# A block table inside the expert loop: gathers and stores by token, queries from SBUF to SBUF, and filler matmuls

## The reference

```python
x = x + gelu(layernorm(x) @ ctx.T) @ ctx                     # 1: context as weights
# 2: eight experts, every token goes to one of them
probs = softmax(xt @ Wg)                                     # xt = layernorm(x), 2048 tokens
top_idx = top_k(probs.T, cap=256)                            # each expert picks 256 tokens
tok2exp = best of the experts that picked the token, or the best of all
out = sum_e where(tok2exp == e, weight, 0) * (gelu(xt @ W1[e]) @ W2[e])
x = x + out
# 3: attention of ctx (keys, values) and layernorm(x) (queries), 16 heads of 16, masked, relative bias
x = x + attention(q = layernorm(x) @ Wq, k = ctx @ Wk, v = ctx @ Wv) @ Wo
# 4: per batch one of eight experts is chosen from the last token, then
x = x' + 0.3 * (expert(x') @ Wo + bo)                        # x' = layernorm(x)
```

## Time and profile before

| | |
|---|---|
| median of 3 runs | 817.16 us (813.94 to 817.80) |
| profiled execution, its own time | 816.39 us |
| its span in the trace | 814.6 us |
| PE busy | 682.0 us, 84% |
| DVE, ACT, POOL busy | 352.0, 271.2, 34.9 us |
| mean granted TensorE clock | 0.904 of full |
| HBM read, written | 50.12 MB, 20.79 MB |

### The profile page before, as it was taken

How to read it: one execution, slowest core, us unless ns; L and a number is a source line. 1 busy time by engine, 2 the same in 40 slices (tenths; PEclk the granted TensorE clock), 3 DMA queues, 4 the chain that set the end, 5 groups by cost and what they waited for, 6 DMA issues and landing times.

```text
span 814.6 us, 8616 instructions
## 1 busy us (share of the span) xinstructions
PE 682.0 (84%) x2992; PEld 370.3 (45%) x2993; DVE 352.0 (43%) x965; ACT 271.2 (33%) x371; POOL 34.9 (4%) x40
## 2 busy tenths in 40 slices
PE   4999999999777226999727888999999998978997
PEld 2666666666554114666512332333333345444455
DVE  4414320030356201222255666777777844525134
ACT  1111111111132101334215313665666654752410
POOL 0000000000100430000070000000000000000000
PEclk9999999999989757999957765999999989989999
DMA  9974019120011153211136931035035100022102
GB/s 312 363 245 169 0 56 375 61 84 0 1 48 48 55 170 99 64 52 60 57 100 119 160 65 41 1 74 105 17 65 114 28 2 1 1 73 83 52 27 77
DMA packets 53547, 71.76 MB, mean 88 GB/s; under 512 B 8498, under 2 KB 46290, under 8 KB 52322
## 3 DMA queue, kind: packets, MB, share of 16 engines
q1 hardware_dynamic: 51970, 67.04, 29.4%
q0 software_dynamic: 1536, 4.20, 1.6%
HBM read 50.12 MB, written 20.79 MB: 87 GB/s over the span
## 4 chain that ended last, share of the span: by engine, by line
PE 66%; DVE 15%; issue 6%; DMA 5%; ACT 4%; SPq 3%; POOL 0%; DVEq 0%; ACTq 0%
PE ps L753 12%; PE ps L764 11%; PE ps L1190 7%; PE ps L1104 6%; DVE arena L1811 6%; PE ps L1171 5%; PE ps L913 4%; DMA arena<-xs_sorted 4%; PE ps L1239 3%; PE ps L1228 3%; PE ps L931 3%; PE ps L726 3%; PE ps L962 2%; PE ps L1251 2%; DVE arena L1592 1%
## 5 line engine op out<-in xcount | busy, mean ns | idle before, releaser
L1811 DVE TENSOR_REDUCE arena<-ps 128x1 f32<-128x416 f32 x256 | 140.7, 587 | 57.3 <-PE ps L1104 54.8
L1407 ACT ACTIVATE arena<-ps 104x1024 f32<-104x1024 f32 x128 | 124.4, 1020 | 81.1 <-PE ps L1171 81.0
L753 PE MATMUL ps<-xnT,arena 128*128 128x512 f32 x208 | 102.4, 618 | 0.9 <-DVE xnT L1477 0.9
L764 PE MATMUL ps<-arena 128*128 128x256 f32 x416 | 98.9, 382 | 0.0
L1104 PE MATMUL ps<-arena 97*128 97x416 bf16 x256 | 88.4, 378 | 11.8 <-DVE arena L1811 5.6
L764 PEld LDWEIGHTS ps<-arena 128*128 128x128 f32 x416 | 80.0, 192 | 33.4 <-issue 25.0
L1278 ACT ACTIVATE arena<-ps 128x512 f32<-128x512 f32 x52 | 31.0, 597 | 175.3 <-PE ps L753 175.3
L1171 PE MATMUL ps<-arena 100*104 100x512 bf16 x256 | 80.8, 405 | 2.3 <-ACT arena L1407 2.2
L1190 PE MATMUL ps<-arena 104*32 104x512 f32 x512 | 71.2, 629 | 0.2 <-ACT arena L1407 0.2
L1104 PEld LDWEIGHTS ps<-arena 97*128 97x128 bf16 x256 | 23.4, 101 | 105.5 <-DVE arena L1811 93.1
L1477 DVE COPY xnT<-ps 128x512 f32<-128x512 f32 x32 | 21.0, 687 | 111.6 <-PE ps L726 111.6
(11 more groups left out here) (186 smaller groups left out, 659.8 us busy)
## 6 DMA issues: line engine op xcount, KB each, us to landing
arena<-in_W SPq DMA_DIRECT2D x16, 512.0 KB, 9.4
arena<-in_ctxT SPq DMA_DIRECT2D x4, 1664.0 KB, 8.1
arena<-in_ctxN SPq DMA_DIRECT2D x4, 1664.0 KB, 13.3
arena<-q_parts SPq DMA_DIRECT2D x48, 128.0 KB
arena<-in_pW SPq DMA_DIRECT2D x8, 512.0 KB, 4.5
xs_sorted<-zero_tile_s SPq DMA_DIRECT2D x1, 3328.0 KB, 20.1
ys_sorted<-zero_tile_s SPq DMA_DIRECT2D x1, 3072.0 KB, 24.5
q_parts<-arena SPq DMA_DIRECT2D x24, 128.0 KB, 1.8
```

What stands on the lines that cost most here:

```text
L753: ins = pe.matmul(ps[:, 4 + k % 2, :], ctxT_s[:, b % 2, c, f * P:f * P + P], xnT[:, c, S * b:S * b + S], start=(c == 0), stop=(c == KC - 1))
L764: ins = pe.matmul(ps[:, b % 2 * 2 + t // 2, t % 2 * D:t % 2 * D + D], hid[:, (k - 2) % 4, t * P:t * P + P], ctxN_s[:, b % 2, f, :], start= ...
L1407: act.activation(pexp2[0:KT, u % 4, :, :], ps[0:KT, 2 + 2 * (u % 2):4 + 2 * (u % 2), :], ACT.Exp).then_inc(f_pe, 1)
L1811: dve.tensor_reduce(cmax2[:, h, j:j + 1], ps[:, place % 2, 0:KF], AX.X, ALU.max).then_inc(f_scu, 1)
```

## The change

1. **Blocks by a table.** `xs_sorted` and `ys_sorted`, their zeroing, the 16 scatters and the 16 gathers go. SP stores the normed rows plainly to `xn_rows` as they come. DVE and PE turn the slots into a table `token_of_slot` (column = block, partition = place in the block, value = token, or `T` for an empty slot). POOL loads each block by that table, and stores each block's answers by token, inside the loop; all empty slots read and write the one extra row `T`. After the loop SP loads the answers with four plain DMAs.
2. **SP no longer takes part in the loop**, so the key stores and loads have nothing of it ahead of or behind them.
3. **Queries SBUF to SBUF**: `q_parts` is not used by `fast_way`; `Q2`'s rows are loaded from `qp` as each part is made.
4. **The order of the start of the attention**: only batch 0's queries come ahead of the maxima, those of batches 1, 2, 3 stand at `j` = 1, 3, 5.
5. **Joint norm roots**: batch 0's roots alone, then the adds of batches 1 to 3, then their roots in one go.
6. **Fillers**: `keep_busy(n)` issues n fp32 matmuls of 256 columns whose result nobody reads, at six places.
7. `total` (16 matmuls of 8 columns) becomes `totals`, one matmul of 128 columns and a DVE reduce, and stands ahead of the prefix.

```diff
+            def keep_busy(n):
+                for _ in range(n):
+                    pe.matmul(ps[:, 0, 0:2 * P], eye, cst[:, 0:2 * P], start=True, stop=True, skip_group_check=True)
...
+            pe.wait_ge(s_res, 4)
+            keep_busy(6)
...
-            prefix(ps[:, 1, 0:NT * E], eq_b)
-            total(ps[:, 1, NT * E:NT * E + E], gt).then_inc(s_gp, 1)
+            totals(ps[:, 1, NT * E:2 * NT * E], gt)
+            prefix(ps[:, 1, 0:NT * E], eq_b).then_inc(s_gp, 1)
...
+            for t in range(NT):
+                if t % (NT // 2) == 0:
+                    pe.wait_ge(s_oh, t // (NT // 2) + 1)
+                ins = pe.matmul(ps[:, 1, 0:2 * IDX], pos_b[:, t, :], tok_b[:, t, :, :].rearrange("p a b -> p (a b)"), ...)
+            ins.then_inc(s_ohp, 1)
+            keep_busy(12)
...
@@ DVE, after the slots are known; IDX = 28, P = 128 @@
-            dve.tensor_copy(slot_i[:, :], r16[:, :]).then_inc(s_slot, 1)
+            ch.step(dve, dve.tensor_copy(pb_i[:, 1, :], r16[:, :]))
+            dve.tensor_scalar(pb_i[:, 0, :], pb_i[:, 1, :], P - 1, None, ALU.bitwise_and)
+            ch.step(dve, dve.tensor_scalar(pb_i[:, 1, :], pb_i[:, 1, :], 7, None, ALU.logical_shift_right))
+            ch.step(dve, dve.tensor_copy(pb[:, :, :], pb_i[:, :, :]))
+            ch.step(dve, dve.tensor_tensor(hot_s_[:, :, :], ... [P, NT, IDX] ..., ALU.is_equal))
+            dve.tensor_scalar(tok_b[:, :, 0, :], hot_s_[:, :, :], cst[:, C_OWN:C_OWN + 1], None, ALU.mult)
+            dve.tensor_tensor(tok_b[:, :, 1, :], hot_s_[:, :, :], ..., ALU.mult)
+            for lo in (0, NT // 2):
+                dve.tensor_tensor(pos_b[:, lo:lo + NT // 2, :], ... [P, NT // 2, P] ..., ALU.is_equal).then_inc(s_oh, 1)
+            dve.wait_ge(s_ohp, 1)
+            ch.step(dve, dve.tensor_scalar(tok_t[:, :], ps[:, 1, IDX:2 * IDX], float(P), float(T), ALU.mult, ALU.add))
+            dve.tensor_tensor(idx[:, :], tok_t[:, :], ps[:, 1, 0:IDX], ALU.add).then_inc(s_idx0, 1)
...
@@ DVE, last in a turn of the loop @@
+                dve.tensor_scalar(idx_x[:, :], idx[:, bass.ds(i * 2 + 4, 2)], 0.0, None, ALU.add)
+                dve.wait_ge(s_ysd, i + 1)
+                dve.tensor_scalar(idx_y[:, :], idx[:, bass.ds(i * 2, 2)], 0.0, None, ALU.add).then_inc(s_idx, 1)
...
@@ POOL @@
+            for j in range(2):
+                load_tokens(j, idx[:, j:j + 1])
+            pool.wait_ge(s_slot, 1)
+            pairs = pool.value_load(be_i[0:1, NBLK:NBLK + 1], min_val=1, max_val=PAIRS)
+            pool.wait_ge(s_xsTr, 2)
+            for j in range(2):
+                load_tokens(j, idx[:, 2 + j:3 + j])
+            with pool.Fori(0, pairs) as i:
+                pool.wait_ge(s_idx, i + 1)
+                pool.sem_inc(s_turn, 1)
+                for j in range(2):
+                    load_tokens(j, idx_x[:, j:j + 1])
+                for j in range(2):
+                    pool.wait_ge(s_eyc, i * 2 + j + 1)
+                    pool.sem_inc(s_turn, 1)
+                    store_answers(j)
+                pool.wait_ge(s_ys, i * 32 + 32)
+                pool.sem_inc(s_ysd, 1)
...
@@ SP, after the loop @@
+            sp.wait_ge(s_xsb, pairs * 32 + 64)
+            sp.sem_inc(s_turn, 1)
+            sp.wait_ge(s_ysd, pairs + 1)
+            sp.sem_inc(s_turn, 1)
+            for b in range(B):
+                sp.dma_start(yg[:, TB * b:TB * b + TB, :], yt_d[S * b:S * b + S, :].rearrange("(t p) d -> p t d", p=P)).then_inc(s_gat[b], 16)
...
@@ SP, queries(b, half) @@
-                    sp.wait_ge(s_qst[i][half], 48 * (b // 2 + 1))
-                    for r, part in enumerate(Q_PARTS):
-                        sp.dma_start(Q2[r * DK:(r + 1) * DK, i, hs, :].rearrange("r h n -> r (h n)"),
-                                     q_d[b, part, half].rearrange("d h n -> d (h n)")).then_inc(f_rows[i][half], 16)
+                    for part, s_part in enumerate((s_q1, s_q2, s_qp)):
+                        sp.wait_ge(s_part, KC * b + half + 1)
+                        for r in range(TERMS):
+                            if Q_PARTS[r] == part:
+                                sp.dma_start(Q2[r * DK:(r + 1) * DK, i, hs, :], qp[:, i, part, half, :]).then_inc(f_rows[i][half], 16)
...
@@ PE, fast_way @@
+                keep_busy(12)
+                pe.wait_ge(s_gat[0], 16)
+                keep_busy(3)
+                pe.wait_ge(s_moe, 1)
+                keep_busy(8)
+                pe.wait_ge(s_lnst, 2 * 0 + 1)
+                keep_busy(4)
                 turn_queries(0)
                 queries(0)
-                turn_queries(1)
-                queries(1)
                 for j in range(8):
-                    if j in (1, 4):
+                    if j in (3, 5, 7):
+                        query_rest(j // 2, 1)
+                    if j in (1, 3, 5):
                         share = AU // 8 // KC ** 2
-                        query_products(2 + j // 4, lambda i: max_products(0, ...))
+                        query_products((j + 1) // 2, lambda i: max_products(0, ...))
                     else:
                         max_products(0, j * AU // 8, (j + 1) * AU // 8)
...
+                    if j in (2, 4, 6):
+                        query_rest(j // 2, 0)
+                    if j in (0, 2, 4):
+                        turn_queries(j // 2 + 1)
...
@@ DVE, after the loop @@
+            def add_all_experts():
+                add_answers(0)
+                dve.wait_ge(s_moe, 1)
+                norm_roots(0)
+                norm_shifts(0)
+                for b in range(1, B):
+                    add_answers(b)
+                dve.wait_ge(s_moe, B)
+                norm_roots(1, B - 1)
+                norm_shifts(1, B - 1)
+                dve.sem_inc(s_lnst, B - 2)
```

220 lines of the change are left out of this document (106 added, 114 removed).

## The result

The changed kernel takes 793.69 us in the median (792.56 to 796.32, 4 runs), the kernel before 816.73 (813.94 to 817.8, 4 runs). The ratio is 0.9728, 95% interval 0.9693 to 0.9762: 2.7% faster. The forecast was 778 with a range of 766 to 792, so the direction was right and the range missed the median by 1.7 us; the gain was 23 us and not 38.

A forecast was written before the change was run, and what follows sets the result against it. The prediction saw the gain between 271 and 501 us, in PE's idle waits and reduced clock, with the expert loop itself bound by PE. Its terms summed to 37.9 us off 816.4, giving 778 us, range 766 to 792.

The forecast's parts named there:

- A: From the slots being known to the first hidden product of the expert loop: 15.5 us earlier (bounds 14.5 and 17).
- B: First turn of the expert loop, 21.9 us before: 11.5 us, so 10.4 us less (bounds 6 and 13).
- C: Other nine turns of the expert loop: PE's wait for the next pair's load goes, 1.7 us less.
- D: End of the expert loop to the first add, 11.6 us before: 2.1 us earlier (bounds 0.6 and 3.7).
- the rival that the circle binds: Expert loop: POOL's circle of loads and stores outlasts PE's turn, by slow landing or VectorE blocking POOL; 787 us, chance 0.15.
- The rival of the empty slots: Expert loop: stores to the one row T go one after the other and landing grows; 824 us, chance 0.05.
- E: Batch 0's roots to the first product for the maxima, 26.7 us before: 12.2 us earlier (bounds 9 and 15).
- F: First product for the maxima to the first scores, 54.0 us before: 4 us more (bounds 0 and 12).
- The rest: From the first scores to the end, 313.7 us: no change in length.
- The third: Rival: gathers wait out the key loads and the third batch's queries cost 10 us, not 4; 789 us, chance 0.13.
- The clock holds: Rival: fillers carry PE through the waits, in the first turn and batch queries, 8.5 us better; 770 us, chance 0.17.

The follow-up runs named there:

- the last kernel: Changed kernel with ScalarE copying the next batch's query columns earlier and fillers in PE's idle stretches of the attention and last 140 us: 773.74 us, 0.9473 of the kernel before.

## Why the prediction was half right

**A and B, right in sum.** The list is complete at 273.80 and not 276.7, and POOL's second issue begins at 276.12, 2.2 us earlier than forecast; the gather then took 7.91 us and not 4.0, and from L897 to L913 it is 1.9 us and not 3.2. The errors cancel (L897 at 284.17, just past the forecast's 281 to 284). The 12 fillers are 24 instructions of 7.99 us, where I had 5 at half clock; they began as much earlier, and end at 281.2 as forecast. The rule from the Trainium skill quoted in A (DMA: Bandwidth & Descriptors, section Queues, rings and completion order) would have made the landing shorter; beside the keys it was 7.91, without them 4.9. Going round packet by packet spared the gather nothing that the runs show. B's 11.5 is what was said, at the mixed clock that was said.

**C and D, right.** PE is busy 76.30 of 77.05 us. POOL's circle never bound: it waits 3.6 us in each turn before its loads, and a turn is 8.46 us (330.32 to 338.78). An indirect issue takes 0.94 to 0.99 us and 0.30 between two, so the rival that the circle binds didn't come true in either form. Whether VectorE can hold POOL's issues up was hardly tested: in a turn the four issues (330.32 to 335.15) stand between VectorE's copies (to 329.5 and from 335.6). The one issue that began in a copy, at 285.07, took 0.94 us like the rest. The rival of the empty slots needed a landing of 7.2 us: the last store's issue began at 377.38, and SP, which waits for its landing, issued its loads at 380.60, 3.2 us later.

**E, 1.9 us too good.** The failing number is "issue and landing some 2 us" for the last load of the first half: it landed 5.22 us after its part. Against these 3.2 us stands the clock, which was fully won back where I had counted half: L946 takes 3.70 us, and 6.18 without the fillers. (The sum took 0.9 for that half, its own words give 1.3.) Twelve loads of 128 KB stand in 8.04 us of issues, and DMA is over its full share:

```profile
402.00:407.00 5.00, 0.12 (x1) 0.14 (x2) 0.82 (x5) 2.10 (x5) 0.00 (x0) 0.77 1.17 121
```

A load that stands alone and a load that is the sixth of a burst aren't the same row. I had the bytes (six times 128 KB) and didn't divide them by any rate: at these 121 GB/s they are 6.5 us. The Trainium skill (DMA: Bandwidth & Descriptors, section Why small descriptors are slow (HBM only)) says that transfers from SBUF to SBUF don't suffer from small pieces; here, with packets of under 2 KB, the share of the engines is at its end with 121 GB/s, and the trace doesn't bear it out. Whether the small pieces or the 16 partitions at a time do it, no run shows.

**F, 6.3 us too good.** The step that failed is "ACT also makes all parts of one batch ahead of the next batch's columns, about 1 us at each of two places". It was the right mechanism at a quarter of its price: with that order turned, the stretch shrinks by 7.8 us, in two measurements. Of these, 3.8 are the waits and 4.0 the clock, which stays at 1.2 GHz for one to three pairs of products longer behind a wait (1.91 us for 1.02) in most profiles, though not in all. I priced the wait from the durations of what it waits for, and the clock behind it at nothing. Since one of the two waits stood in the kernel before, not all of the 7.8 can be charged to the change, and a second step failed with it: "Some of the clock is won back. I take 4". My own terms were 6.0 for the third batch and 2 for the waits; I took 4 off them for the clock, and it rose only from 0.66 to 0.69. How the missing 6.3 divide between the two steps, no run shows.

**The rest, 6.8 us, where I said "the change adds and removes nothing there".** It adds and removes nothing, and the length moved all the same. Over the profiles of all kernels without fillers in it the last stretch took 308.4 to 320.6 us, with the granted clock between 0.92 and 0.96, and the changed kernel alone has both 310.8 and 320.5. Dips stand behind PE's idle stretches of 1.67 and 2.6 us in some of these profiles and not in others. In the last kernel, with the stretches filled, the dips right behind them are gone, and its runs agree within 1.2 us. The earlier trace rows had the clue: a clock of 0.95 over 313.7 us with PE 91% busy means dips, and I took it for a constant. Why one idle stretch is followed by a dip in one execution and not in the next is open. A term of 7 us either way for this would have held the result; in the lower set of times the changed kernel is at 783 to 787, inside the range and still 5 to 9 us over the forecast, which are F and E.

**The rivals.** The third (keys and third batch eat more, 789) was the nearest: F grew by 10.3, its number, for another reason, and the keys did hold the gathers up, by 3 us. "The clock holds" was right in E alone (3.70 us for L946). In B the fillers end 3.0 us before the transposes, and L913 runs at half clock; with the keys late, where nothing lies between, it takes 3.69. In F there are no fillers.

## What to carry to other kernels

When work is moved so that one engine serves it in order, write that engine's list of instructions out and look which of them another engine waits for; a copy that TensorE waits for goes ahead of one that only a DMA waits for. Price an idle stretch of TensorE with what may follow it at half clock, here from nothing to as much again as the wait itself. And before a small difference is explained, run the unaltered kernel again: its two sets of times, 9 us apart, were further apart than most parts of this change are worth.
